# A twelve-layer decoder on one core: staggering the two groups at six layer borders, and moving the gate bias of the second expert layer

## What is computed

```python
x = x + sum over the 2 chosen e of gw[e] * (gelu(xn @ W1[e] + b1[e]) @ W2[e] + b2[e])
```

## Time and profile before

| | us |
|---|---|
| median of 3 runs | 700.14 |
| the profiled execution | 699.31 |
| its span, first to last instruction | 697.5 |
| TensorE busy (matmuls) | 546.0 (78%) |
| VectorE busy | 467.8 (67%) |
| ScalarE busy | 258.2 (37%) |
| GpSimd busy | 98.6 (14%) |
| mean granted TensorE clock | 0.918 of full speed |

### The profile page before, as it was taken

One profiled execution on the slowest core, in us unless ns is written; L12 is line 12 of the kernel. 1 busy time (PEld: TensorE's weight loads), 2 busy tenths in 40 slices (PEclk: granted clock), 3 DMA queues, 4 the chain that ended last, 5 costly groups with the idle time before them and its releaser, 6 DMA issues.

```text
span 697.5 us, 10675 instructions
## 1 busy us (share of the span) xinstructions
PE 546.0 (78%) x4265; PEld 374.0 (54%) x4265; DVE 467.8 (67%) x1200; ACT 258.2 (37%) x420; POOL 98.6 (14%) x101
## 2 busy tenths in 40 slices
PE   1426589786899789959997878897879977988477
PEld 0425255576455646556775755555535564556335
DVE  7688788577488567754346635885453468876685
ACT  2355445314354334424332442453312114453270
POOL 5021210015310141010002015100200012102120
PEclk9967699978899999997998999999789989999879
DMA  9800000000000000000000000000000000000001
GB/s 290 353 0 2 0 2 1 1 1 1 0 2 1 1 1 2 1 1 1 0 2 1 1 0 1 1 2 1 0 1 0 1 0 1 2 1 1 0 0 31
DMA packets 6720, 12.40 MB, mean 18 GB/s; under 512 B 528, under 2 KB 4880, under 8 KB 6288
## 3 DMA queue, kind: packets, MB, share of 16 engines
q1 hardware_dynamic: 6672, 11.73, 4.7%
HBM read 11.21 MB, written 0.52 MB: 17 GB/s over the span
## 4 chain that ended last, share of the span: by engine, by line
PE 63%; DVE 23%; ACT 8%; POOL 2%; issue 2%; DMA 1%; SPq 0%; DVEq 0%; ACTq 0%
PE ps L391 46%; PE ps L444 10%; ACT big L884 5%; PE ps L407 3%; DVE st L1149 3%; DVE big L1260 3%; PE ps L460 2%; DVE mx L1256 2%; DVE xn L1343 2%; POOL rs L326 2%; DMA co<-in_ctx 1%; DVE mv L1152 1%; DVE x L1273 1%; PE ps L573 1%; DVE ve L1154 1%
## 5 line engine op out<-in xcount | busy, mean ns | idle before, releaser
L884 ACT ACTIVATE big<-ps 128x1024 f32<-128x1024 f32 x80 | 81.9, 1023 | 114.8 <-PE ps L444 114.8
L1256 DVE TENSOR_REDUCE mx<-ps 128x8 f32<-128x1024 f32 x80 | 97.5, 1219 | 34.0 <-PE ps L391 34.0
L1260 DVE TENSOR_TENSOR big<-ps,mx 128x1024 f32<-128x1024 f32 x80 | 98.0, 1225 | 7.3 <-DVE mx L1256 0.5
L444 PE MATMUL ps<-kt,big 128*128 128x128 f32 x640 | 85.7, 277 | 17.3 <-DVE big L1260 17.3
L444 PEld LDWEIGHTS ps<-kt,big 128*128 128x128 f32 x640 | 70.7, 141 | 52.4 <-DVE big L1260 43.1
L326 POOL TENSOR_TENSOR rs<-ve,negh 128x4 f32<-128x4 f32 x26 | 26.6, 1023 | 401.5 <-DVE ve L1154 401.5
L391 PE MATMUL ps<-xnT,wt 128*128 128x512 f32 (+1 forms) x140 | 74.6, 670 | 3.1 <-DVE big L1535 3.1
L391 PEld LDWEIGHTS ps<-wt,big 128*128 128x128 f32 (+1 forms) x480 | 56.0, 191 | 10.3 <-issue 8.6
L391 PE MATMUL ps<-wt,big 128*128 128x128 f32 (+1 forms) x480 | 60.1, 279 | 0.8 <-ACT big L1039 0.8
L391 PE MATMUL ps<-big,vaug 128*32 128x128 f32 x1280 | 51.5, 279 | 10.6 <-ACT big L884 10.6
L343 POOL TENSOR_TENSOR KTm<-qk,kt 128x512 f32<-128x512 f32 x34 | 37.4, 1109 | 107.3 <-PE ps L391 67.2
(11 more groups left out here) (274 smaller groups left out, 770.8 us busy)
## 6 DMA issues: line engine op xcount, KB each, us to landing
wt<-in_weights SPq DMA_DIRECT2D x1, 1664.0 KB, 16.0
wt<-in_weights SPq DMA_DIRECT2D x1, 1603.0 KB, 10.9
wt<-in_weights SPq DMA_DIRECT2D x6, 256.0 KB, 10.1
bt<-in_bconsts SPq DMA_DIRECT2D x1, 1024.0 KB, 7.6
rowt<-in_rows SPq DMA_DIRECT2D x1, 975.0 KB, 5.4
wt<-in_weights SPq DMA_DIRECT2D x1, 832.0 KB, 12.3
wt<-in_weights SPq DMA_DIRECT2D x1, 608.0 KB, 17.3
wt<-in_weights SPq DMA_DIRECT2D x1, 580.0 KB, 5.4
```

Of the source, the lines that this page charges most:

```text
L444: ins = pe.transpose(heads_of(pair(g, u % 2))[:, j // HG, j % HG, :], pr[:, (u % 2) * HH + j, :], ident)
L884: act.activation(PT[:, half * HH:(half + 1) * HH, :].rearrange("p (i j) k -> p i j k", i=2), heads_of(pair(g, half)), ACT.Exp, scale=SCALE ...
L1256: dve.tensor_reduce(top, S, AX.X, ALU.max).then_inc(*s.step())
L1260: dve.tensor_tensor(pr[:, half * HH:(half + 1) * HH, :].rearrange("p (i j) k -> p i j k", i=2), S, top.unsqueeze(3).to_broadcast([P, 2, HG ...
```

## The change

Three things:

1. **Staggered borders**, for L0f, L1x, L1f, L2x, L2f and L3x (`BEHIND`). The head of such a layer for group 0 (variance, root, xn, values, first keys, and on TensorE the projections of keys and values) gets keys inside the layer before, on beat 9 of attention (for L2x: 35.x of L2a). The tail of group 0 moves forward: `back` to key 99, ahead of group 1's second half of the last sequence (100); `normal` to 103 and 104; the transposes and copy of the output projection to 108; its matmuls to 121; `add` to 120. Group 1's `back(1)` and `back(3)` go behind group 0's matmuls (122). In the new layer group 1's blocks get keys behind group 0's (4.1 to 4.7, 5.5 in L0f and L2f, 10.5 in L1f). Each of the five attentions is followed by a layer of `BEHIND`; the border of L1f to L2a, and those into L0x, L1a, L3a and L3f, keep their order.
2. **The wait** of GpSimd's key spreading in L1x and L2x for the xn of both groups becomes one for its own group's.
3. **L1f**: `turn_gates` and `gate_bias` move from before `hidden(1)` to behind `hidden(2)` (24.5 and 26.5), with ScalarE's copy between. On ScalarE group 0's exponentials (7.8) and its first two Gelu (7.9) go ahead of group 1's exponentials (8).

No arithmetic is added or taken away. Lines beginning with - are the kernel before.

```diff
@@ -257,0 +258,6 @@
+    BEHIND = {"L0f": 5.5, "L1x": 4.5, "L1f": 10.5, "L2x": 4.5, "L2f": 5.5, "L3x": 4.5}
+
+    def ahead(n, l, k):
+
+        return n - 1, (35 + k / 10 if l == "L2x" else beat(2 * GB + 1, k))
+
@@ -332 +338,4 @@
-                    yield n, ((1 + b if first == 0 else 19) if b < 2 else beat(2 * (b - 2) + g))
+                    if g == 0 and b == 0 and l in BEHIND:
+                        yield ahead(n, l, 6)
+                    else:
+                        yield n, ((1 + b if first == 0 else 19) if b < 2 else beat(2 * (b - 2) + g))
@@ -339,2 +348 @@
-                            for other in range(GROUPS):
-                                pool.wait_ge(*s.at(f"{l}.xn", other))
+                            pool.wait_ge(*s.at(f"{l}.xn"))
@@ -357 +365 @@
-                yield n, 0
+                yield (ahead(n, l, 2) if g == 0 and l in BEHIND else (n, 0))
@@ -472 +480 @@
-                    yield n, 4
+                    yield n, (4.7 if g and l in BEHIND else 4)
@@ -476 +484 @@
-                yield n, 20
+                yield n, (4.6 if g == 0 and l in BEHIND else 20)
@@ -498 +506 @@
-                yield n, beat(2 * GB + g)
+                yield n, (beat(2 * GB - 1, -1) if g == 0 else beat(2 * GB + 1))
@@ -500,0 +509,2 @@
+                if g == GROUPS - 1:
+                    yield n, beat(2 * GB + 1, 2)
@@ -506 +516 @@
-                yield n, 130
+                yield n, (beat(2 * GB - 1, 8) if g == 0 else 130)
@@ -509 +519 @@
-                yield n, 131
+                yield n, (beat(2 * GB + 1, 1) if g == 0 else 131)
@@ -524 +534 @@
-            def turn_gates(n, l, k):
+            def turn_gates(n, l, k, phase):
@@ -526 +536 @@
-                yield n, 12
+                yield n, phase
@@ -543 +553 @@
-                    yield n, 0
+                    yield (ahead(n, l, 3) if g == 0 and l in ("L1x", "L2x", "L3x") else (n, 0))
@@ -549,0 +560,2 @@
+                        if l in BEHIND:
+                            yield (ahead(n, l, 3) if g == 0 else (n, 4.1))
@@ -561 +573 @@
-                    yield n, 2
+                    yield n, (BEHIND[l] if g and l in BEHIND else 2)
@@ -637 +649 @@
-                    yield n, 3
+                    yield n, (4.65 if g and l in BEHIND else 3)
@@ -653 +665 @@
-                            yield from turn_gates(n, l, E0)
+                            yield from turn_gates(n, l, E0, 12)
@@ -669,2 +680,0 @@
-                    yield from turn_gates(n, l, E1)
-                    yield from gate_bias(n, l, E1, w("L1f_b2", E1), 14)
@@ -674,0 +685,3 @@
+                        if e == 1:
+                            yield from turn_gates(n, l, E1, 24.5)
+                            yield from gate_bias(n, l, E1, w("L1f_b2", E1), 26.5)
@@ -905 +918,4 @@
-                    yield n, 1
+                    if l in BEHIND:
+                        yield (ahead(n, l, 3) if g == 0 else (n, 4.1))
+                    else:
+                        yield n, 1
@@ -923 +939 @@
-                yield n, 2
+                yield n, ((7.85 if l == "L1f" else BEHIND[l]) if g and l in BEHIND else 2)
@@ -975 +991 @@
-                    yield n, 5
+                    yield n, (4.05 if g == 0 and l in BEHIND else 5)
@@ -987 +1003 @@
-                    yield n, 8
+                    yield n, (7.8 if l == "L1f" and g == 0 else 8)
@@ -992 +1008 @@
-                            yield n, 11
+                            yield n, (7.9 if g == 0 else 11)
@@ -995,3 +1010,0 @@
-                    if l == "L1f":
-                        yield n, 13
-                        read(t.gwTT[0:k, :], bank(3)[0:k, :], "gwTp", "gwT")
@@ -1012 +1025,4 @@
-                        yield n, 16 + 4 * e
+                        if i == 4:
+                            yield n, 24.5
+                            read(t.gwTT[0:E1, :], bank(3)[0:E1, :], "gwTp", "gwT")
+                        yield n, 16 + 4 * e + (0.7 if e == 2 else 0)
@@ -1053 +1069 @@
-                    yield n, 5
+                    yield n, (4.05 if g == 0 else 5)
@@ -1246 +1262 @@
-                    yield n, 3
+                    yield (ahead(n, l, 6) if g == 0 and l in BEHIND else (n, 3))
@@ -1262 +1278 @@
-                yield n, beat(2 * GB + g, 2)
+                yield n, beat(2 * GB + (-1, 1)[g], 3)
@@ -1264 +1280 @@
-                yield n, beat(2 * GB + g, 3)
+                yield n, beat(2 * GB + (-1, 1)[g], 4)
@@ -1336 +1352,2 @@
-                yield n, 0
+                early = g == 0 and l in BEHIND
+                yield (ahead(n, l, 1) if early else (n, 0))
@@ -1340 +1357 @@
-                yield n, 1
+                yield (ahead(n, l, 5) if early else (n, 1))
@@ -1473 +1490 @@
-                    yield from add(n, l, 3 - 3 * g)
+                    yield from add(n, l, 3 - 3 * g, phase=(beat(2 * GB + 1), 200)[g])
@@ -1519 +1536 @@
-                    yield from add(n, l, 0, "y2")
+                    yield from add(n, l, 0, "y2", phase=(35, 200)[g])
@@ -1579 +1596 @@
-                    yield n, 3
+                    yield (ahead(n, l, 6) if g == 0 else (n, 3))
```

## The result

The changed kernel took 690.27 us, the median of 4 runs (688.47 to 691.29), against 699.95 for the kernel before beside it: a ratio of 0.9867 (0.9849 to 0.9885). The forecast was 683.0 within 677 to 692. The direction and the range held, but the narrower range that the forecast gave itself, 679 to 688, did not; of the 17.1 us forecast 9.2 came, by the profiled executions (spans of 697.5 and 688.3).

What follows compares the result with a forecast made beforehand. The prediction saw a chain (TensorE 63%, VectorE 23%) loose at the borders between layers. Gains 1.5 + 4.2 + 4.1 + 3.4 + 3.3 + 0.6 = 17.1 us gave 683.0 us against the median of 700.14, range 677 to 692.

Steps and rivals of the forecast that it cites:

- L0f: Border from L0x into L0f: gain 1.5 us, bounds 0.7 if the clock falls and 2.4 if it holds.
- L1f: Head of L1f: earlier group 0 work and the moved gate bias, with three table loads, gain 4.1 us.
- L3x: Head of L3x: group 0's lead mostly lost behind group 1's transposes and q; gain 0.6 us, bounds 0 and 1.1.
- L2x: Border from L2a into L2x: first maxima at 429.75 instead of 433.18, gain 3.4 us.
- L1x: Head of L1x: first maxima at 247.1 instead of 251.27, gain 4.2 us.
- L2f: Head of L2f: gain 3.3 us, bounds 2.3 if the clock falls and 7.0.
- The border step by step: End of L0x: group 1's transposes start 0.5 us late, group 0's next head starts 3.15 us earlier.
- group 1 gains nothing at a border: Border after L0x: group 1's xn is done at 143.8 us, before 143.7.
- The floor of 1.5: L1f: the least gain in us, if another 2.6 us of ScalarE time came on the path.
- The clock holds everywhere: Rival, all borders: every upper bound is reached, gain 22.2 us, so 678 us; chance 0.2.
- Group 1 sets the pace: Rival, all heads: each moves only as far as group 1's, gain 8.1 us, so 692 us; chance 0.17.
- Slower: Rival: 0.5 us delay at five attentions plus L1f's two loads cost 5.1 us, so 705 us; chance 0.06.

Runs made afterwards that it cites:

- a1_again: The changed kernel run once more with nothing edited: 689.02 us (685.96 to 691.56).
- e1_ctx_only: The changed kernel with only the borders into L1x, L2x and L3x staggered and the early Gelu undone: 695.21 us.
- e4_fill: The changed kernel plus matmuls that nobody reads in TensorE's holes at the borders into L0f, L1f and L2f: 683.77 us.
- e2_gates_back: The changed kernel with L1f's gate transposes and gate bias back ahead of hidden(1): 690.06 us.
- e5_no_L3x: The changed kernel with the border into L3x in the old order: 689.64 us.
- e3_exp_first: The changed kernel with both groups' exponentials before all Gelu in L1f, one table load instead of three: 686.01 us.
- e7_best: The changed kernel with L3x's border in the old order, exponentials first in L1f, and fillers at the borders into L0f, L1f and L2f: 682.87 us.
- e6_before_fill: The kernel before, nothing staggered, plus five unread matmuls in TensorE's hole at the borders into L0f, L1f and L2f: 695.11 us.
- e8_L0f_turn: The changed kernel with group 1's transposes and gates in L0f ahead of group 0's expert products (key 4.5 for 5.5): 689.22 us.
- e10_clean: The changed kernel with L0f key 4.5, L3x's group 1 keys and values earlier, and exponentials first in L1f, no fillers: 691.27 us.
- e11_all: e10_clean plus the fillers at the borders into L0f, L1f and L2f: 683.01 us.

## Why the prediction was right and wrong

The forecast was 17.1, the profile shows 9.2. The gap of 7.9 is L0f 4.3, L1f 2.2, L3x 2.6, L2x 0.4, L1x 0.1 and 0.6 in other stages, less 2.3 that L2f brought above its forecast. The mechanism of the two context layers was right. That the total stayed in the wide range is owed in part to luck: without L2f's surplus of 2.3 us the total would have been 692.6, outside it.

- **The border step by step** held. Group 1's last subtraction starts 0.53 later in this profile (127.05 for 126.52; 0.19 of it is the later start of L0x), and behind it the last `turned` of group 1 starts at 128.58, 0.25 late instead of 0.5; the hole is 2.74 for 2.8; "group 1 gains nothing at a border" is right (its root starts at 141.51 before and at 141.86 in a1_again; here, with the output matmuls at half clock, at 143.49).
- **L1x** (4.2, measured 4.1) and **L2x** (3.4, measured 3.0) were right for the reason given: keys and values of the context fill the hole, VectorE waited for group 0. The sign "I am wrong if they gain under 2.5 each" did not come, and e1_ctx_only shows the gain by itself.
- **L0f** is the step that failed: "Then L0f gains 0.7" was the lower bound for a clock that falls. I had the clock fall and recover earlier by the same stretch, and forgot that the stretch then lies over group 1's own chain, which before ran at full speed, and that group 0's matmuls stand in front of group 1's logits at half speed. I had those logits at 149.1; they came at 152.71. The stage gained -2.8 where the clock fell at 137 and 1.1 where it did not (a1_again). The upper bound, 2.4, was not reached either: in e4_fill, with the border filled, the gain is 1.2, and 1.3 went into the 32 slow matmuls behind the wait for gw. In all the profiles with this border staggered the stage gains between -3.2 (e2_gates_back) and 1.4, and in each the clock falls somewhere in it, so none shows what it takes at full clock.
- **L1f**: the term of 4.1 was for a full clock, though the border has the same hole as L0f's. 4.0 in e4_fill and in e5_no_L3x, where the fall came behind the gates of both groups, 1.9 in the changed kernel, where it lay over them, from 308 to 315. This was a mechanism that I used two paragraphs later and did not carry over. The part on the table loads held: each is 1.28 us and the next activation begins 0.01 us behind it (318.61 + 1.28 = 319.89, the exponential at 319.90). The Trainium skill (ScalarE: Activation LUTs, "What ACT_TABLE_LOAD costs") gives some 2.66 us per switch with the drain; no such drain shows between two activations here, and taking two of the loads away changed the stage by 0.3 us (e3_exp_first, 56.39, against a1_again, 56.70). The trace was the better choice, though L1f fell short for another reason. The floor of 1.5 was passed by the changed kernel by little.
- **L2f** gave 5.6 with a forecast of 3.3 and bounds of 2.3 to 7.0. In the changed kernel the clock stayed at full speed through its hole, and the first fall lasted from 488.6 to 492 where before it lasted from 490.7 to 501. Counted from the root, the routing block starts at 8.71 (492.61) instead of 13.14 (503.02), 4.4 earlier; the forecast was 4.2 for a clock that holds. The other 1.2 is the second fall, which before made eight matmuls last 6.57: it is shorter, not gone, and they last 5.40. At full speed they last 3.70 (e2_gates_back, at 501.29), so 3.9 was read too high. The timeline of the changed kernel in L2f:

```profile
479.20 0.66 PE L415 MATMUL ps<-kt,co 128*128 128x128 f32 x4 [2.74 <-DVE co L1255]
...
491.09 0.69 DVE L1552 TENSOR_TENSOR big<-ps,big 128x512 f32<-128x512 f32 x1 [2.23 <-ACT big L1067]
...
492.61 0.18 DVE L1559 TENSOR_SCALAR lg<-lgm 128x64 f32<-128x64 f32 x1
...
498.42 5.40 PE L399 MATMUL ps<-xnT,wt 128*128 128x512 f32 x8 [2.80 <-DVE big L1552]
```

  The same 2.74 us hole as in L0f, and here the four transposes behind it take 0.66: full speed. That fall and hole do not go together by their length alone is plain from these two rows.
- **L3x** was forecast at 0.6 within 0 to 1.1 and lost 2.0. I had seen that group 0's scores wait for group 1 there, so the lead buys nothing, but had not asked what stands ahead of group 1: its keys and values (key 4.1) come in front of its transposes, which start 1.64 us after its xn is ready. That is the whole of the 1.5 between root and scores in this profile. (Before, they started at 642.06, 3.02 behind the root, as soon as their xn was there.) In a1_again, where the keys and values ran at full clock, the transposes start 2.97 behind the root, no later than before; the clock fell behind them, q of group 1 took 1.89 us and not 1.13, and the scores came at 6.00 for 5.32. So the step that I had not priced costs what the clock makes of it. The rest lies behind the scores, where the order is the same as before: 16.53 us from scores to the next root before, 17.01 in the changed kernel, 17.88 in a1_again, and 17.57 in e7_best with the old order. Before, the clock fell at 651.2 there, 12.1 us behind the root; in the three others 11.0 to 11.4 behind it, so over more of the following matmuls. e6_before_fill, also with the old order, takes 23.60, with a mean granted clock of 0.68 from 636 to 640. So the clock can cost as much here as the order does.
- **The rivals.** "The clock holds everywhere" (678) fell in the changed kernel; with fillers at three borders the time is 683.8, but the clock falls in L0f, L1f, L2f and L3x even so, and no run here has what this rival supposes. "Group 1 sets the pace" (692) is closer to the measured total (690.27) than the forecast is, and wrong in its cause: L1x and L2x have group 0's full lead. "Slower" decided in L3x alone, and by another queue than the one I named.
- **Readings.** The window 142 to 143 with 0.79 puts the first fall at 142.6, not 142.8, which is where TensorE starts again; the one with 0.90 puts the second at 507.8. Nothing in the sum hangs on either.

Open: why the clock falls behind the same hole in one execution and not in another; the long fall in L1f of e8_L0f_turn and e10_clean; the 1 to 1.5 us by which L2a differs between kernels (54.4 to 55.9); and GpSimd's shorter wait by itself, which was not tried: with the new order of its queue the longer one would wait for a block queued behind it.

## What to carry to other kernels

A stagger paid what the timeline says where other work fills the hole that it leaves (L1x, L2x), and paid differently from one execution to the next where it does not: behind a hole of 2.74 us the following chain ran at half clock in one execution and at full clock in another. So work it out at both clocks over everything behind it, group 1's chain too, before taking it as a gain. Where a hole can't be filled with real work, a few matmuls that nobody reads can be worth as much as a good part of the reordering (5.3 to 6.5 us here on top of 9.7). And compare stage by stage: a total that moved by 4 us (e3_exp_first) had moved in a stage that the edit did not touch.

## What was not expected of the hardware

- The same program, with the same hole of 2.7 us, was granted 0.53 or 1.00 at 137 us in two executions; the two profiles differ by 4 us of 690 in that stage, where all its eight runs spread over 5.6 (685.96 to 691.56).
- An execution that kept its clock at 137 lost it a little later, at 153 in a1_again, at 154 in e4_fill and, with the same fillers, at 143 in e11_all; and with another order in L0f it was low for 21 us in L1f (301 to 322), in two kernels.
- VectorE's xn of one group takes 1.11 us alone and 1.87 beside a GpSimd product (628.49 for 1.09, in L3x of the changed kernel). The kernel before had it in L3x as well (3.13 for both groups' xn at 638.87, where the border into L0f has 2.36), so it moved nothing here.
